# Moving degrees and neighbourhood aggregation from the layer stage into the recurrent stage

## What is computed

```python
A_hat = A + jnp.eye(N)
d = jnp.sum(A_hat, axis=2)
d_inv = jnp.where(d > 0, d_safe ** (-0.5), 0.0)
A_norm = d_inv[:, :, None] * A_hat * d_inv[:, None, :]
...
dyn = conv1d(x, conv_w) + conv_b          # 3 taps
lw = lstm(dyn, w_ih, w_hh, b_ih, b_hh)    # 128 steps
agg = jnp.matmul(A_norm, x)
out = jax.nn.sigmoid(jnp.matmul(agg, lw))
```

## Time and profile before

| | |
|---|---|
| median of three runs | 1939.26 us (1936.72 to 1941.2) |
| profiled execution, its own time | 1942.61 us |
| its span, first to last instruction | 1940.4 us |
| mean granted TensorE clock | 0.787 of 2.4 GHz |
| layer stage, groups under way | about 1016 to 1483 us |
| recurrent stage | about 1489 to 1887 us |
| output stage | about 1887 to 1940 us |

### The profile page before, as it was taken

How to read it: one execution, slowest core, us unless ns; L and a number is a source line. 1 busy time by engine, 2 the same in 40 slices (tenths; PEclk the granted TensorE clock), 3 DMA queues, 4 the chain that set the end, 5 groups by cost and what they waited for, 6 DMA issues and landing times. The chain is left out here.

```text
span 1940.4 us, 38226 instructions
## 1 busy us (share of the span) xinstructions
PE 1560.5 (80%) x8862; PEld 1292.8 (67%) x8862; DVE 1292.3 (67%) x5372; ACT 1004.8 (52%) x2174; POOL 733.5 (38%) x1312
## 2 busy tenths in 40 slices
PE   4888888888888888888854766567667999999995
PEld 3777777777777777777753544455555777777774
DVE  5777777778778787777745888888873222222227
ACT  3777776777777777777741222222221333333337
POOL 4444444444444444444433566556652000000006
PEclk9988898889999999898976777887787555555558
DMA  3322233222232222222200000000000000000002
GB/s 80 89 67 65 70 73 73 70 65 67 74 78 68 65 74 75 70 67 65 71 23 10 22 23 22 11 22 22 28 11 1 0 0 0 0 0 0 0 0 88
DMA packets 140443, 82.82 MB, mean 43 GB/s; under 512 B 64963, under 2 KB 136031, under 8 KB 140385
## 3 DMA queue, kind: packets, MB, share of 16 engines
q1 hardware_dynamic: 138660, 81.06, 16.3%
q10 hardware_dynamic: 1725, 1.13, 0.2%
HBM read 77.31 MB, written 4.82 MB: 42 GB/s over the span
## 5 line engine op out<-in xcount | busy, mean ns | idle before, releaser
L676 PEld LDWEIGHTS wf<-w2t,hid 128*128 128x128 f32 x1536 | 351.6, 315 | 40.0 <-issue 28.6
L676 PE MATMUL wf<-w2t,hid 128*128 128x128 f32 x1536 | 374.4, 401 | 1.9 <-DVE hid L878 1.9
L860 DVE SCALAR_TENSOR_TENSOR msg<-wf,val_sq,rfe 128x128 f32<-128x128 f32 x768 | 210.3, 344 | 134.7 <-PE wf L676 129.7
L501 POOL TENSOR_TENSOR xb<-xin,bd2bc 128x128 f32<-128x128 f32 x64 | 29.2, 456 | 494.2 <-DVE xres L850 494.2
L692 PE MATMUL rg<-rf_hi,pick 128*128 128x128 bf16 x768 | 157.9, 239 | 29.6 <-issue 29.1
L580 ACT ACTIVATE rfe<-rg 128x768 f32<-128x768 f32 x128 | 102.6, 802 | 133.5 <-PE rg L692 127.4
L1532 DVE SCALAR_TENSOR_TENSOR r_new<-r_gates 128x64 f32<-128x64 f32 x128 | 28.8, 225 | 205.9 <-ACT r_gates L1514 205.9
L692 PE MATMUL rg<-rf_mid,pick 128*128 128x128 bf16 x768 | 158.0, 239 | 0.0
L692 PE MATMUL rg<-rf_lo,pick 128*128 128x128 bf16 x768 | 157.6, 239 | 0.0
L1583 POOL MEMSET r_minus_half<- 128x4 f32 x1 | 0.1, 101 | 410.5 <-POOLq L1456 410.5
L1482 PEld LDWEIGHTS r_zgi<-xin,w_hh 128*128 128x128 f32 x508 | 118.1, 320 | 50.9 <-issue 43.5
(11 more groups left out here) (271 smaller groups left out, 4208.8 us busy)
## 6 DMA issues: line engine op xcount, KB each, us to landing
val_bc<-edge_val SPq DMA_DIRECT2D x256, 96.0 KB, 2.7
idx_bc<-edge_idx SPq DMA_DIRECT2D x128, 192.0 KB, 3.0
adj_w<-in_adj_rows SPq DMA_DIRECT2D x64, 64.0 KB, 2.5
xt_w<-in_x_cols SPq DMA_DIRECT2D x64, 64.0 KB, 2.1
adjt_w<-in_adj_t SPq DMA_DIRECT2D x64, 64.0 KB, 1.9
xin<-in_x_rows SPq DMA_DIRECT2D x32, 128.0 KB, 2.1
m_adj_g<-in_adj_rows SPq DMA_DIRECT2D x16, 256.0 KB, 2.8
m_adjt_g<-in_adj_t SPq DMA_DIRECT2D x16, 256.0 KB, 2.8
```

Of the source, the lines that this page charges most:

```text
L676: last = pe.matmul(column(wf, r), h[:, r, :], w2t[:, :], start=True, stop=True)
L860: last = dve.scalar_tensor_tensor(msg[:, q, r * P:(r + 1) * P], column(wf, r), val_sq[:, q4, r:r + 1], rfe[:, q, r * P:(r + 1) * P], ALU.m ...
```

## The change

The layer stage loses `deg`, `dsafe`, `dpos`, `dpow`, `dinv`, `xs`, `adj_i`, the aggregate and the load of the transposed adjacency. The recurrent stage gets them, in 32 quads of four steps; quad Q loads two graphs' transposed adjacency and forms their degrees, and multiplies the aggregate of the two graphs of quad Q-1. The degrees are now matmuls of the adjacency (as weights) with one column of ones. The identity is no longer added by POOL; it is a second matmul into the same sum. All steps are written out, so no hardware loop and no register address is left in that stage. The diff, cut to its core:

```diff
@@ layers12
-                            after(sp, "adj_i", g, -4)
-                            load_t(g, -2)
-                            pool.tensor_tensor(adj_i[:, :, :], adjt_g[:, g.mod(2, -3), :, :],
-                                               ident[:, :].unsqueeze(1).broadcast_to((P, G, P)), ALU.add)
-                            pool.tensor_scalar(dsafe[:, :], deg[:, g.mod(2), :], 1.0, 1.2e-38, ALU.add, ALU.max)
-                            pool.tensor_scalar(dpos[:, :], deg[:, g.mod(2), :], 1.0, 0.0, ALU.add, ALU.is_gt)
-                            pool.tensor_tensor(dpow[:, :], dsafe[:, :], minus_half[:, :], ALU.pow)
-                            pool.tensor_tensor(dinv[:, four(g)], dpow[:, :], dpos[:, :], ALU.mult)
-                            evac(g, -3, agg[:, four(g, -3), :], ph[:, :, :], "agg_p", "agg")
-                            for j in range(G):
-                                last = pe.matmul(ph[:, j, :], xs[:, j, :], adj_i[:, j, :], start=True, stop=True)
-                            dve.tensor_tensor(xs[:, :, :], xres[:, four(g, -3), :], bc(dinv[:, four(g, -3)]), ALU.mult)
-                            dve.tensor_reduce(deg[:, g.mod(2), :], adj_g[:, g.mod(2), :, :], AX.X, ALU.add)
@@ lstm, SP and POOL, for Q in range(QUADS)
+                    before(sp, agg_p, 2 * (Q - 1))
+                    sp.dma_start(adjt[:, Q % 2, :, :], a["adj_t"][:, 2 * Q:2 * Q + 2, :])
+                    pool.wait_ge(deg_copied, Q + 1)
+                    pool.tensor_scalar(dsafe[:, :], deg_b_copy[:, Q % 2, :], 1.0, 1.2e-38, ALU.add, ALU.max)
+                    pool.tensor_scalar(dpos[:, :], deg_b_copy[:, Q % 2, :], 1.0, 0.0, ALU.add, ALU.is_gt)
+                    pool.tensor_tensor(dpow[:, :], dsafe[:, :], half[:, :], ALU.pow)
+                    pool.tensor_tensor(dinv[:, 2 * Q:2 * Q + 2], dpow[:, :], dpos[:, :], ALU.mult)
+                    pool.tensor_tensor(xs[:, Q % 2, :, :], xres[:, 2 * Q:2 * Q + 2, :],
+                                       dinv[:, 2 * Q:2 * Q + 2].unsqueeze(2).broadcast_to((P, 2, P)), ALU.mult)
@@ lstm, PE
+                def aggregate(Q, j):
+                    i = j // 2
+                    if j % 2 == 0:
+                        pe.wait_ge(xs_ready, Q + 1)
...
+                        pe.sem_inc(held["PE"], 1)
+                        pe.matmul(agg_b[i], xs[:, Q % 2, i, :], adjt[:, Q % 2, i, :], start=True, stop=False)
+                    else:
+                        pe.matmul(agg_b[i], xs[:, Q % 2, i, :], ident[:, :], start=False, stop=True)
+                def degrees(Q):
+                    pe.wait_ge(adjt_in[Q % 2], 16 * (Q // 2 + 1))
+                    before(pe, agg_ready, 2 * (Q - 1))
+                    pe.sem_inc(held["PE"], 1)
+                    for i in range(2):
+                        last = pe.matmul(deg_b[:, i:i + 1], adjt[:, Q % 2, i, :], k["ones"][:, 0:1],
+                                         start=True, stop=True)
+                for t in range(P):
+                    Q, j = t // 4, t % 4
...
+                        recurrence(t, hs[:, t - 1, :])
+                    if Q + 1 < QUADS:
+                        inputs(4 * (Q + 1), order[j])
+                    if Q >= 1:
+                        aggregate(Q - 1, j)
+                    if j == 1:
+                        degrees(Q)
+                for j in range(4):
+                    aggregate(QUADS - 1, j)
@@ lstm, ACT, behind tanh_c of step t
+                    if j % 2 == 0 and t >= 6:
+                        keep_aggregate((t - 6) // 2)      # copies one 128x128 aggregate
+                    if j == 1:
+                        act.activation(deg_b_copy[:, Q % 2, :], deg_b, ACT.Copy)
```

More of the change, by code:

```diff
@@ L95, in build @@
         all_idx = nc.dram_tensor("all_idx", [ALL_UNITS, P * R], BF16, kind="Internal").ap()
-        held = {n: ctx.enter_context(nc.semaphore("held_" + n)) for n in ("SP", "DVE", "Pool", "ACT")}
+        held = {n: ctx.enter_context(nc.semaphore("held_" + n)) for n in ("SP", "DVE", "Pool", "ACT", "PE")}
         w_ih, w_hh = sb("w_ih", [P, 4, P]), sb("w_hh", [P, 4, P])
@@ L1108, in body @@
                             rstd_of(g, -1, "n1")
[L1109 to L1127, removed]
                         if two:
@@ L1297, in body @@
                     for g, one, tail, two, three in steps(pair):
[L1298 to L1302, removed]
-                            dve.tensor_tensor(xs[:, :, :], xres[:, four(g, -3), :], bc(dinv[:, four(g, -3)]), ALU.mult)\
-                                .then_inc(s["xs"], 1)
                         if one:
@@ L1454, in z_of @@
             return z_o[bank][:, 0:2, :].rearrange("p a (t b) -> p (a t) b", b=B)
+        QUADS = P // 4
+        adjt = sb("adjt", [P, 2, 2, P])
+        xs = sb("xs", [P, 2, 2, P])
+        dsafe, dpos, dpow, half = (sb(n, [P, 2]) for n in ("dsafe", "dpos", "dpow", "half"))
+        adjt_in = [sem(f"adjt_in{i}") for i in range(2)]
+        half_ready, deg_p, dsafe_ready, dpos_ready, dpow_ready, dinv_ready, xs_ready, agg_p, agg_ready = (
+            sem(n) for n in ("half_ready", "deg_p", "dsafe_ready", "dpos_ready", "dpow_ready", "dinv_ready",
+                             "xs_ready", "agg_p", "agg_ready"))
@@ L1477, in inputs, with recurrence @@
                               skip_group_check=True)
-                def recurrence(bank, j, h):
+                def recurrence(t, h):
                     for q, ready in ((G_, None), (I_, zgi_ready), (F_, zf_ready), (O_, zo_ready)):
-                        last = pe.matmul(z_of(bank, q)[:, j, :], w_hh[:, q, :], h, start=False, stop=True,
+                        last = pe.matmul(z_of(t // 4 % 2, q)[:, t % 4, :], w_hh[:, q, :], h, start=False, stop=True,
                                          skip_group_check=True)
@@ L1523, in _ @@
+                for n in range(B - 3, B):
+                    keep_aggregate(n)
             @block.vector
@@ L1557, in lstm, with reached @@
         lwt_b = [z_o[i][:, :, :] for i in range(2)]
-        o_b = [c0.enter_context(nc.psum_tensor(f"r_o{i}", [P, G, P], F32)) for i in range(2)]
         NGR = B // G
         ON_DVE = G // 2
-        def before(eng, name, count):
+        def reached(eng, name, count):
             if count > 0:
@@ L1607, in _ @@
                     if g < NGR:
-                        before(pe, "lw_ready", g - 1)
+                        reached(pe, "lw_ready", g - 1)
                         for j in range(G):
```

198 lines of the change are left out of this document (102 added, 96 removed).

## The result

The changed kernel takes **2002.07 us** (median of 4 runs, 2000.39 to 2003.52) against 1937.99 us before (4 runs, 1932.61 to 1941.2): ratio 1.0333, 95% interval 1.0307 to 1.0359. It is slower by 3.3%. The profiled execution took 2003.52 us, its span is 2001.5 us.

The account below looks back on a forecast made before the run. PE bounds the recurrent stage at the low clock, DVE the layer stage. Profiled 1942.6 + 77 (recurrent) - 11 (layer) = 2008.6, less 3.3 to the median: 2005 us, slower by 3.4%, range 1980 to 2028.

Parts of the forecast that it names:

- The clock falls in the first steps and stays low: Recurrent stage: clock drops to 0.50 from the third or fourth step and the added PE work does not raise it.
- would need luck: Recurrent stage: said of a run whose clock does not fall in steps 0 to 3, needed for about 1835 us.
- +77 in the recurrent stage: PE-bound steps at the low clock lengthen to 3.51 us, plus 0.86 per quad for two one-column degree matmuls: +77 us.
- The hidden parts: Recurrent stage: ACT's copies, POOL's five operations a quad and SP's loads run beside the steps and cost nothing.
- rival (3): Recurrent stage: semaphore increments or late `xs` hold PE up beyond its work; +10 to +20, 2015 to 2025 us; chance 0.10.
- The semaphore increments, taken as nothing: Recurrent stage: PE's increments ahead of aggregates and degrees, 96 in all, cost 0 to 10 us; forecast took 0.
- -11 in the layer stage: Layer stage gets 11 us shorter, between 0 and -22, as DVE loses `xs` and its other losses gain nothing.
- DVE loses `xs` ... where DVE waits for nothing: 16 x 0.69 = 11 us: Layer stage: removing `xs` from the head of DVE's turn saves its full 0.69 us in each of 16 groups.
- POOL and ACT lose work that DVE does not wait for: Layer stage: work taken from POOL and ACT gains nothing, since DVE, the bound, does not wait for it.
- the degree sum would be absorbed: Layer stage: DVE's degree sum, 0.67 us a group, turns into a longer wait at the score; gain nothing.
- Rival (1): Recurrent stage: aggregates keep the clock up, steps 2.26 and 2.55 us, stage -93, total 1835 us; chance 0.17.
- Rival (2): Recurrent stage: added PE work is hidden even at the low clock because the engine ring sets the step; 1925 us; chance 0.03.

Follow-up runs that it names:

- e1: Changed kernel plus one unread 128-column matmul in each of steps 0 to 3, which have no aggregate yet; 1824.14 us, ratio 0.9417 to the kernel before.
- e6: e1 without the three unread 512-column matmuls just ahead of the recurrent stage (WARM = 0); 2002.44 us, ratio 1.0343 to the kernel before.
- e4: Changed kernel with one two-column degree matmul per quad in place of two one-column ones, output wrong; 1986.99 us, ratio 1.0264 to the kernel before.
- e12: Changed kernel plus one burst of eight unread 384-column matmuls ahead of step 12's aggregate; 1839.65 us, ratio 0.9487 to the kernel before.
- e3: Changed kernel without the work moved into the recurrent stage, aggregates and degree factors constant, output wrong; 1922.62 us, ratio 0.9925 to the kernel before.
- e8: e1 with the degree sum on DVE and POOL's four degree operations kept in the layer stage; 1838.78 us, ratio 0.9487 to the kernel before.
- e9: e8 with POOL's four degree operations done once for all graphs at the recurrent stage's start; 1824.28 us, ratio 0.9405 to the kernel before.
- e10: e8 with DVE's degree sum cut from 128 columns to one, degrees incomplete; 1840.03 us, ratio 0.9494 to the kernel before.
- e5: Kernel before, nothing moved, plus one unread 128-column matmul in each of steps 0 to 123; 1858.91 us, ratio 0.9595 to the kernel before.
- e11: e5 with the steps written out in place of the hardware loop; 1838.79 us, ratio 0.9484 to the kernel before.
- e2: Kernel before with the recurrent steps written out and nothing moved; 1932.78 us, ratio 0.9977 to the kernel before.

## Why the prediction was right

Forecast 2005 (1980 to 2028), measured 2002. Its terms, one by one:

- **The clock falls in the first steps and stays low.** Right: 0.99 for four steps, then 0.50 over 450 us. That the first four steps decide is now shown by e1 (filled: 1.00 to the end), and by e6 that the same filled steps can stay at either clock. The 8 runs of the changed kernel and of e4 all lie where only a low clock puts them (1979 us or more). But e12, whose first steps are the same, kept the clock in its profiled execution. So "would need luck" was borne out, and some luck is in the forecast too: its main term rests on something that varies from one execution to the next.
- **+77 in the recurrent stage.** Measured +71.3 and 1.7 behind it, **+73**. The step was forecast at 3.51 and is 3.50, the degree step at 4.37 and is 4.35; quads 1 to 30 took 445.2 us instead of 447.0. The one-column matmul was taken at the upper bound, 0.43, and e4 shows 0.42. The clock lasted two steps longer than I took (-1.6), the first degree pair was hidden (-0.9), and the tail was 1.7 instead of 1.1. In e3 the same work costs 79 by the medians and 77 by the profiles. Two small slips: the first four distances before are 10.3 us and not 10.7, and the bounds that the prediction lists add up to 1962 to 2026, not 1980 to 2028, unless the 27 us for the one-column matmul are left out in part.
- **The hidden parts, and rival (3).** Right: PE waited for neither `xs` nor `adjt`. The semaphore increments, taken as nothing, leave no time in a step of 3.50. Rival (3), which had PE held up by them or by `xs`, did not come.
- **-11 in the layer stage.** Measured -15.2, and the term came near by luck, because two errors cancelled. The step "DVE loses `xs` ... where DVE waits for nothing: 16 x 0.69 = 11 us" failed: in e8 it is gone, and the wait of the later operation `xin<-m_pa,m_rsum` is 19.8 us where the same line waited 8.5 before, so as much as the 11.1 us came back there. The step "POOL and ACT lose work that DVE does not wait for" failed as well: without taking away POOL's four operations there is no gain (e8), with it there are 14.8 us (e9), since in part they push POOL's large operations into DVE's way. That the degree sum would be absorbed was right but for 3.3 us at most (e10).
- **Rival (1)**, 1835 us. Its place and mechanism are those of e1, which measured 1824. Its degree step was forecast at 2.55 and is 2.35: the degree pair takes 0.37 and not 0.46, and from input to aggregate it is 1610.83 - 1610.29 = 0.54 and not 0.63. The rule of "TensorE: Matmul & The Clock Gate" of the Trainium skill, Part 1 (The HAM clock gate), that a busy PE releases the low clock, does not hold here if busy means having records, as the prediction said: 0.50 with records for 465.58 of 466 us in e6.
- **Rival (2)** is refuted by e4, where 0.42 us less on PE shortens the step by 0.42.

## What to carry to other kernels

Where a ring of engines keeps TensorE in short pauses, ask first which clock each stretch is granted and in which state it begins: the same steps ran at 2.26 or 3.50 us, and four unread matmuls at the right place were worth 178 us, more than anything that was moved. Work moved beside such a ring is nearly free at the high clock and costs its full length at the low one, so price it at both before choosing. An operation counts as "waited for by nobody" only if nothing behind it on its engine is waited for either. Look, too, at what it pushes back: that may then run beside a short operation of the engine that bounds the stage, and lengthen it.

## What the hardware showed that was not expected

- Two self-holding states: the same instruction stream of 128 steps keeps 1.00 for 287 us or 0.50 for 466 us, by the state at its start (e1, e6).
- At 1.2 GHz an f32 matmul of 1, 64 or 128 columns behind others costs the same 0.42 to 0.43 us (0.42 by e4; the earlier trace rows), at 2.4 GHz the one-column one 0.37 / 2 = 0.18.
- The hardware loop with its register addresses costs 0.19 us a step in a latency-bound ring at 2.4 GHz (e5 against e11, 20 us in all), and 0.04 at 1.2 GHz.
- A 128x4 operation on DVE that starts while a 128x512 one runs on POOL ends with it: 0.94 us instead of 0.17, and up to 1.29 (e8, e9).
- The clock of unfilled steps fell after 2 steps of 2.26 us (before, e3) or 23 (e2). With the changed kernel's first four steps it fell after the fourth (after) or the third (e4), and not at all in e12's profiled execution.
